# Preparation's inputs loaded one stage ahead, its order on VectorE and ScalarE anew, and the closing stage's selecting products behind its first tile

## The chip, the cores and the metric

The kernel runs on one core of one Trainium2 chip. The metric is the device time of one launch in microseconds, the median of several runs. Engines are named as in the profile: PE (TensorE matmul), PEld (its weight load), DVE (VectorE), ACT (ScalarE), POOL (GpSimd), SP (SyncE, which issues all DMAs here).

## What is computed

A mixture of experts, then three attention blocks, each added to its input `x`, which has 2 x 1024 rows of 256 floats.

```python
x = x + moe(x, cond_64, ...)                       # 8 experts, top 2, and 2 shared ones
x = x + rel_attn(x, mask_f, ..., null_kv=cond_64)  # layer 1
x = x + bias_attn(x, fside, mask_k, ...)           # layer 2
x = x + rel_attn(x, mask_f, ..., null_kv=cond_64)  # layer 3

def rel_attn(x, mask, ...):
    xn = ln(x, g_norm)
    q = l2norm(heads(xn @ Wq)) * q_scale           # 16 heads of 64
    k, v = split(xn @ Wkv)                         # one head of keys and values
    k, v = concat([null_k, k]), concat([null_v, v])
    k = l2norm(k) * k_scale
    h = silu(ln(pos @ w0 + b0, g0))                # a small network over 1024 distances
    h = silu(ln(h @ w1 + b1, g1)) @ w2 + b2        # gives the bias of each distance and head
    sim = q @ k.T * 8 + [null_attn_bias, h[i - j]]
    return ln(softmax(causal(sim, mask)) @ v @ Wout, g_out)
```

`bias_attn` is the same without the norms of q and k and without the small network: its bias is the input `fside`.

## The kernel before, in words

`program` (L2048) runs phases one after the other, each closed by a barrier of all engines: `moe_route`, `moe_experts`, and then for layers 1, 2 and 3 `prepare_layer`, `project`, `attend` and `close_layer`. Within a phase every engine has its own list of instructions, written out by hand, and semaphores order them; nothing of a phase starts before the slowest engine of the one before has reached the barrier. `Own` is a helper with which DVE waits for its own results.

`prepare_layer` (L583) makes what the projections need: the weights `Wq` and `Wkv` multiplied by `g_norm` (`fold` on ACT, L908; L737 on DVE), each split into a high and a low part (`wq_h` L911, `wq_l` L709, `wx_h` L761, `wx_l` L763); the products of `Wq` with the null key (`null_products`, L702) and their sums per head (`null_columns`, L758); the mask's penalty row (L726, L728); and the first 512 rows of `x` normalized, transposed and split (`first_rows` L828, `first_standardize` L841, `first_transposes` L694, L917, `first_low` L849). In layers 1 and 3 (`normed`) it also runs the small network over the 1024 distances, in quarters m = 0 to 3: two halves of the first layer, then two of the second. `distances` (L768) or `add_first_bias` (L774), `variances` (L781 to L788), `deviation` on ACT (L924), `offsets` (L793, L795), `normalize` on ACT (L932), transposes on PE (L989), `tangent` on ACT (L942), `silu` (L801), `high_silu` on ACT (L950), `low_silu` (L807), products on PE (L216). The last DVE instruction (L895) writes the bias row `brow`, SP stores it and issues the DMA that spreads it out in DRAM (L683), and the barrier follows.

Its inputs are loaded by SP at the phase's start (L646): 26 DMAs in a normed layer, 11 in layer 2. DVE's list starts with the first 512 rows of `x`, which need none of them.

`attend` (L1508) ends with DVE, ACT and PE idle and SP waiting until its stores of the attention's output, `o_dram`, have landed (L1660). The first of four chunks of that output has been loaded into `o_in` by then (`load_outputs`, L1501).

`close_layer` (L1851) multiplies the output by `Wout`: 16 tiles of 128 rows, four in a chunk. A tile: ACT makes the high part (L1914), DVE the low part (L1971), PE 48 products (L216), a transpose of the null weights (L1956), and one product for the null value (L1963), which needs ACT's copy of that transpose (L1932). ACT prepares tile n + 2 while PE is at tile n. That null product needs `null_out`, which comes from eight products with the raw `Wout` (`cl_vps`, L1943, the selecting products), the first thing that PE does in the phase. The raw `Wout` lies in the buffer of the second chunk, so SP waits for them before it loads chunk 1. It loads chunk c, from 2 on, when DVE has made the low parts of chunk c - 2, whose buffer it takes.

`moe_experts` (L387) loads the weights of two experts, then in a loop of four turns four blocks of `fside` (`load_corners`) that POOL masks (L514) between its low parts (L519).

## Time and profile before

| what | value |
|---|---|
| median of 3 runs | 2287.53 us (2285.26 to 2294.27) |
| the profiled execution | 2292.38 us, of which its span 2290.6 us |
| mean granted TensorE clock | 0.934 |
| PE busy | 1975.9 us (86%) |
| DVE busy | 1694.2 us (74%) |
| ACT busy | 1341.0 us (59%) |
| POOL busy | 1071.1 us (47%) |

Times of the trace are microseconds from the span's start. The phases that the change touches lie in these stretches: experts 32 to 219, preparation of the three layers 220 to 283, 936 to 960 and 1572 to 1635, closing stages 872 to 935, 1510 to 1571 and 2218 to the end. A row of a timeline has the start, the duration (of several instructions together where xN stands), engine, line, operation, the tiles written and read, and in brackets how long the engine was idle before it and what ended that.

### The profile page before, as it was taken

What the parts mean: (1) busy time and instruction counts of PE and PEld (TensorE: products, weight loads), DVE (VectorE), ACT (ScalarE), POOL (GpSimd) and SP (SyncE); (2) the same over time, 40 slices, a digit from 0 to 9 for tenths busy, and PEclk for the clock granted to TensorE, in tenths of its full rate; (3) what the DMA queues carried; (4) which work ended last, traced back from release to release, by engine and by line L of the source; (5) the groups of instructions that cost most, each with busy time, mean ns of one, the idle gap of its engine ahead of it and who ended that gap; (6) DMA issues with size and microseconds to landing.
All of it is one profiled execution on the core that took longest, in us unless ns stands there. A gap on an engine that the chain in (4) does not pass through costs nothing. (4 is left out here: it accounts for less than half of the span.)

```text
span 2290.6 us, 46788 instructions
## 1 busy us (share of the span) xinstructions
PE 1975.9 (86%) x11698; PEld 1428.0 (62%) x11698; DVE 1694.2 (74%) x4116; ACT 1341.0 (59%) x2908; POOL 1071.1 (47%) x1289
## 2 busy tenths in 40 slices
PE   5998496899999999488999999985686999999987
PEld 4886364666666668466666666675464666666667
DVE  5777767777887785657777877758487778887856
ACT  2222465677776674246766767643564777777753
POOL 1442113666765562105656666521123666666632
PEclk8999698899999999798999999997796999999999
DMA  3530167433333333286777877741464433343332
GB/s 114 170 129 18 47 212 254 118 112 111 111 112 110 100 113 120 77 315 195 240 230 237 240 239 238 230 157 39 142 217 161 125 111 110 111 121 114 111 111 98
DMA packets 220689, 338.83 MB, mean 148 GB/s; under 512 B 25910, under 2 KB 102844, under 8 KB 220508
## 3 DMA queue, kind: packets, MB, share of 16 engines
q1 hardware_dynamic: 220508, 336.86, 46.8%
q8 instruction: 60, 0.98, 0.2%
q14 instruction: 121, 0.99, 0.1%
HBM read 250.63 MB, written 102.91 MB: 154 GB/s over the span
## 5 line engine op out<-in xcount | busy, mean ns | idle before, releaser
L1569 POOL TENSOR_SCALAR at_row<-at_row,at_inv 128x129 f32<-128x129 f32 (+7 forms) x384 | 721.3, 1878 | 353.9 <-DVE at_inv L1731 346.5
L1778 ACT ACTIVATE at_row<-at_row,at_nmax 128x129 f32<-128x129 f32 (+7 forms) x768 | 595.4, 775 | 231.9 <-DVE at_nmax L1750 230.5
L1750 DVE CUSTOM_DVE_ANT_0 at_row<-at_s,bias,at_row 128x128 f32<-128x128 f32 (+7 forms) x768 | 618.4, 811 | 69.2 <-PE at_s L1678 38.0
L1690 PE MATMUL at_t<-ident,at_row 128*128 128x128 f32 x3456 | 546.1, 282 | 37.6 <-ACT at_pt L1771 32.6
L1690 PEld LDWEIGHTS at_t<-ident,at_row 128*128 128x128 f32 x3456 | 394.0, 142 | 242.4 <-issue 165.5
L1677 PE MATMUL at_s<-k_hh,q_hl 128*128 128x512 f32 (+3 forms) x1152 | 464.5, 403 | 47.6 <-SPq L1636 22.1
L1706 PE MATMUL at_o<-at_pt,v 128*64 128x512 f32 (+3 forms) x2304 | 442.5, 506 | 6.1 <-ACT at_pt L1771 2.5
L1584 DVE COPY at_pt<-at_t 128x128 f32<-128x128 f32 (+3 forms) x576 | 278.4, 483 | 188.7 <-PE at_t L1690 188.5
L1678 PE MATMUL at_s<-k_lp,q_h 65*128 65x512 f32 (+3 forms) x1152 | 393.6, 354 | 0.0
L1771 ACT ACTIVATE at_pt<-at_t 128x512 f32<-128x512 f32 (+2 forms) x576 | 306.8, 533 | 139.7 <-PE at_t L1690 134.0
L1677 PEld LDWEIGHTS at_s<-k_hh,q_hl 128*128 128x128 f32 x1152 | 226.3, 196 | 81.7 <-DVE at_nmax L1750 35.2
L1706 PEld LDWEIGHTS at_o<-at_pt,v 128*64 128x64 f32 x2304 | 144.7, 138 | 182.6 <-issue 146.3
L1569 DVE TENSOR_SCALAR at_row<-at_row,at_inv 128x129 f32<-128x129 f32 (+7 forms) x384 | 248.8, 648 | 0.9 <-DVE at_inv L1731 0.6
L1678 PEld LDWEIGHTS at_s<-k_lp,q_h 65*128 65x128 f32 x1152 | 226.7, 197 | 16.7
L1474 POOL TENSOR_TENSOR o_in<-pj_qn,o_in 128x512 fp32r<-128x512 f32 x38 | 52.7, 1390 | 213.3 <-ACT o_in L1233 213.3
L1778 ACT ACTIVATION_READ_ACCUMULATOR at_row<-at_row,at_nmax 128x1 f32 x768 | 143.9, 187 | 0.0
L1833 POOL COPY null_w<-at_row 128x2 f32 (+1 forms) x384 | 71.3, 186 | 137.3 <-DVE at_row L1569 74.3
L1821 POOL COPY at_row<-neg_null 128x2 f32 (+1 forms) x384 | 71.3, 187 | 126.5 <-DVEq L145 103.6
L519 POOL TENSOR_TENSOR moe_hid_l<-moe_hid,moe_hid_h 128x512 fp32r<-128x512 f32 x40 | 51.8, 1294 | 145.5 <-ACT moe_hid_h L504 145.5
L216 PE MATMUL cl_y<-wo_h,cl_oh 128*128 128x256 f32 x384 | 114.0, 297 | 0.0
L216 PE MATMUL cl_y<-wo_l,cl_oh 128*128 128x256 f32 x384 | 109.1, 284 | 0.0
L216 PE MATMUL cl_y<-wo_h,cl_ol 128*128 128x256 f32 x384 | 109.1, 284 | 0.0
(244 smaller groups left out, 2832.6 us busy)
## 6 DMA issues: line engine op xcount, KB each, us to landing
q_dram<-o_in SPq DMA_DIRECT2D x96, 512.0 KB, 3.7
q_hl<-q_dram SPq DMA_DIRECT2D x192, 256.0 KB, 4.4
bias<-bands_dram SPq DMA_DIRECT2D x64, 512.0 KB, 5.8
q_h<-q_dram SPq DMA_DIRECT2D x96, 256.0 KB, 5.2
o_dram<-at_o_sb SPq DMA_DIRECT2D x96, 256.0 KB, 4.7
o_in<-o_dram SPq DMA_DIRECT2D x10, 2048.0 KB, 8.6
bands_dram<-brow_dram SPq DMA_DIRECT2D x2, 8192.0 KB, 31.6
bias<-corners_dram SPq DMA_DIRECT2D x256, 64.0 KB, 4.3
```

The lines of the kernel that those rows point to most:

```text
L216: last = eng.matmul(out, left[a], right[b], start=start and n == 0, stop=stop and n == len(pairs) - 1)
L1569: return eng.tensor_scalar(cells, cells, inv[:, i:i + 1], None, ALU.mult)
L1584: copy(bass.AP(one.tensor, one.offset, [one.ap[0], [pitch, blocks], [1, P]]), t_ps[m % NTR][:, 0:blocks * P].rearrange("p (c i) -> p c i", ...
L1677: eng.matmul(out, q_hl[:, g % 2, side, at], t["k_hh"][:, b, c:c + n], start=True, stop=False)
L1678: last = eng.matmul(out, q_h1[0:DH + 1, g % 2, side, at], t["k_lp"][0:DH + 1, b, c:c + n], start=False, stop=True)
L1690: last = eng.transpose(t_ps[m % NTR][:, c * P:(c + 1) * P], row[:, u % RING, here:here + P], t["ident"][:])
L1706: last = eng.matmul(o_ps[side * DH:(side + 1) * DH, i0:BANK], t["v"][:, turn.half_of(GU * g) * NT + j, :], pt[g % 2][:, side, at + i0:at + ...
L1750: eng.tensor_tensor_reduce(out=row[:, u % RING, ZERO:ZERO + width], in0=s_ps[u % 2][:, 0:width], in1=bt[:, lo:lo + width], scale=-1.0, sca ...
L1771: return eng.activation(out, in_, ACT.Copy)
L1778: eng.activation(cells, cells, ACT.Exp, scale=-1.0, bias=nmax[:, i:i + 1], accum_out=rsum[:, i:i + 1]).then_inc(s["exp"], 1)
L1821: eng.tensor_copy(null_cell(u, 2), nulls(turn, "neg_null", u)).then_inc(s["null_in"], 1)
L1833: eng.tensor_copy(nulls(turn, "null_w", u), null_cell(u, 2)).then_inc(s["null_out"], 1)
```

## The change

1. `load_inputs` is new. SP issues the loads of the next `prepare_layer` from the phase before: those of layer 1 in `moe_experts`, between the first two experts' weights and the loop; those of layers 2 and 3 in `close_layer`, between the loads of chunk 1 and chunk 2. They go into the lower half of the bias buffer, which is allocated once for all layers now, and into small tiles of their own. `dist` is loaded once, in `moe_route`.
2. `prepare_layer`: ACT folds `Wq` first. DVE in layers 1 and 3 starts with the network, does the rows of `x` where it would wait for ACT's tanh, the mask, the null values and `wx` after the last `offsets`, and `null_columns` at the very end. The ones of `q_h1` (L862) are written in layer 1 alone, between `low_silu(2)` and `silu(3)`. In layer 2 the low part of `Wq` (L709) goes from DVE to POOL.
3. `close_layer`: the selecting products come behind PE's first tile, and the null product of tile 0 into the middle of tile 1.
4. `attend` doesn't wait for its last two stores; SP waits for them at the start of `close_layer`.

```diff
+def load_inputs(eng, t, w, cond, mask, layer):
+    i, normed = t["inputs"], layer != 2
+    def load(dst, src):
+        eng.dma_start(dst, src).then_inc(t["inputs_sem"], 16)
+        t["inputs_n"] += 16
+    if normed:
+        for n in ("w0", "b0"):
+            load(i[n], rows(w[n]))
+        for n in range(2):
+            load(i[f"g{n}"][:], w[f"g{n}"])
+        load(i["w1"], ...)
+        load(i["w2"][:], ...)
+        load(i["b2"][:], ...)
+        load(i["b1"], rows(w["b1"]))
+    load(i["wq"], w["Wq"].rearrange("(k p) n -> p k n", p=P))
+    load(i["gain"][:], w["g_norm"])
...
 # moe_experts, SP
                     load(eng, q, q)
+                load_inputs(eng, t, *inputs)
                 with eng.Fori(0, NU // PAR - 1) as it:
 # prepare_layer, POOL
             def _(eng):
+                loaded(eng)
                 if normed:
                     null_products(eng)
-                    low_part(eng)
+                low_part(eng)
 # prepare_layer, DVE
+                loaded(eng)
                 if not normed:
+                    null_square()
+                    first_rows()
+                    cleared()
+                    null_values()
+                    first_standardize()
+                    null_products(eng)
                     first_low()
-                    null_key()
-                    null_products(eng)
-                    low_part(eng)
                     null_columns()
                     xo.settle()
                     return
-                eng.wait_ge(s["rb_in"], 16 * 9)
+                null_square()
+                rb.step(eng.memset(w2[:], 0.0))
                 rb.settle()
+                rb.step(eng.tensor_copy(w2[:, :, 0:H], i["w2"][:]))
                 distances(0)
                 variances(0)
-                first_low()
                 distances(1)
+                offsets(0)
                 variances(1)
-                offsets(0)
                 offsets(1)
+                first_rows()
                 split_weights()
+                first_standardize()
                 silu(0)
                 low_silu(0)
                 silu(1)
                 low_silu(1)
+                first_low()
                 null_key()
-                for i in range(2):
-                    add_first_bias(i)
-                    variances(2 + i)
-                    offsets(2 + i)
+                rb.step(eng.memset(brow[:], -BIG))
+                add_first_bias(0)
+                variances(2)
+                add_first_bias(1)
+                offsets(2)
+                variances(3)
+                offsets(3)
+                cleared()
+                null_values()
+                for m in range(2):
+                    silu(2 + m)
+                    low_silu(2 + m)
+                    if m == 0:
+                        ones()
                 null_columns()
-                for i in range(2):
-                    silu(2 + i)
-                    low_silu(2 + i)
 # prepare_layer, ACT, layers 1 and 3
+                fold()
...
                 deviation(0)
+                normalize(0)
                 deviation(1)
-                normalize(0)
                 normalize(1)
+                first_deviation()
...
-                fold()
+                first_high()
+                high_part()
                 deviation(2)
+                normalize(2)
                 deviation(3)
-                normalize(2)
                 normalize(3)
 # attend, SP
-                    eng.wait_ge(s[f"o{g}"], 8 * NGRP * B * TURNS + 16)
+                    eng.wait_ge(s[f"o{g}"], 8 * NGRP * B * TURNS)
 # close_layer, SP
+                eng.wait_ge(t["o_stored"], t["o_stored_n"])
                 for c in range(1, NCH):
+                    if c == 2 and inputs is not None:
+                        load_inputs(eng, t, *inputs)
                     if c >= 2:
                         eng.wait_ge(s["o_lo"], CT * (c - 1))
                     else:
                         eng.wait_ge(s["null_mm"], 1)
 # close_layer, PE (null_rows: the eight selecting products; null_product: the product of L1963)
-                for a in range(NPAIR):
-                    last = eng.matmul(vps[:, 0:D], ...)
-                last.then_inc(s["null_mm"], 1)
                 for n in range(NTT):
                     eng.wait_ge(s["o_lo"], n + 1)
...
                         if a == NPAIR // 2:
+                            if n == 1:
+                                null_product(0)
                             eng.wait_ge(s["w_low"], 3)
...
+                    if n:
+                        null_product(n)
+                    else:
+                        null_rows()
```

Where the instructions stand, at the three places that the prediction speaks of. In rows of after, `bias` stands for the inputs and for the network's `h` and `z`, which all lie in that buffer.

DVE at the end of the preparation of layer 1, before, from the last statistics of the network on:

```order
L788 TENSOR_SCALAR rb_rstd<-rb_mv 128x4
L793 RECIPROCAL rb_rstd<-rb_rstd 128x4
L795 SCALAR_TENSOR_TENSOR rb_off<-rb_mv,rb_rstd 128x4
L758 TENSOR_REDUCE lw_wx<-lw_prod 128x16 x2
L761 CAST wx_h<-lw_wx 128x512
L763 TENSOR_TENSOR wx_l<-lw_wx,wx_h 128x512
L801 SCALAR_TENSOR_TENSOR o_in_4<-o_in_4,rb_tr_6 128x512 x2
L807 TENSOR_TENSOR rb_ul<-o_in_4,rb_uh 128x512 x2
L801 SCALAR_TENSOR_TENSOR o_in_4<-o_in_4,rb_tr_6 128x512 x2
L807 TENSOR_TENSOR rb_ul<-o_in_4,rb_uh 128x512 x2
L895 TENSOR_SCALAR rb_brow<-rb_mm,rb_b_6 16x1024
```

The same place after:

```order
L755 CAST lw_pen<-in_mask_0 2x1024
L757 TENSOR_SCALAR lw_pen_r<-lw_pen 2x1024
L761 COPY v0m<-in_v_0 64x8 x6
L766 TENSOR_SCALAR bias<-bias,in_gain 128x192 x2
L815 SCALAR_TENSOR_TENSOR o_in_0<-o_in_0,rb_tr_5 128x512 x2
L821 TENSOR_TENSOR rb_ul<-o_in_0,rb_uh 128x512 x2
L877 MEMSET q_h_0 1x512 x4
L815 SCALAR_TENSOR_TENSOR o_in_0<-o_in_0,rb_tr_5 128x512 x2
L821 TENSOR_TENSOR rb_ul<-o_in_0,rb_uh 128x512 x2
L772 TENSOR_REDUCE bias<-lw_prod 128x16 x2
L775 CAST wx_h<-bias 128x512
L777 TENSOR_TENSOR wx_l<-bias,wx_h 128x512
```

The mask and null values have come behind the last statistics, the memsets between the last two quarters, and the null columns (L758 to L763 of before, L772 to L777 of after) from ahead of the last silu to behind it.

PE at the start of the closing stage of layer 1, before (`cl_y0` is the result of tiles 0, 2, ..., `cl_y1` that of 1, 3, ...):

```order
L1706 MATMUL at_o_8<-at_pt1_8,v_4 64x128 x2
L81 UNCONDITIONAL_BRANCH
L1940 UNCONDITIONAL_BRANCH
L1943 MATMUL cl_vps_9<-o_in1_4,v0m_4 96x256 x8
L216 MATMUL cl_y0_9<-wo_h_4,cl_oh_9 128x256
L216 MATMUL cl_y0_9<-wo_l_4,cl_oh_9 128x256
```

After, the end of tile 0 and the start of tile 1:

```order
L216 MATMUL cl_y0_9<-wo_h_7,cl_oh_9 128x256
L216 MATMUL cl_y0_9<-wo_l_7,cl_oh_9 128x256
L216 MATMUL cl_y0_9<-wo_h_7,cl_ol_9 128x256
L1993 MATMUL cl_vps_9<-o_in1_0,v0m_0 96x256 x8
L216 MATMUL cl_y1_9<-wo_h_7,cl_oh_9 128x256
L216 MATMUL cl_y1_9<-wo_l_7,cl_oh_9 128x256
```

The eight selecting products now stand between tiles 0 and 1, and tile 0 is PE's first work of the phase.

SP in the closing stage of layer 1, before:

```order
L1505 DMA o_in_4<-o_dram 128x8x512
L1597 DMA o_dram<-at_o_sb 128x512 x4
L81 UNCONDITIONAL_BRANCH
L1884 UNCONDITIONAL_BRANCH
L1505 DMA o_in_4<-o_dram 128x8x512 x3
```

After:

```order
L1547 DMA o_in_0<-o_dram 128x8x512
L591 DMA bias<-in_L_Wq 128x2x1024
L591 DMA in_gain<-in_L_g_in 128x2
L591 DMA in_k_0<-in_cond 128x64
L591 DMA bias<-in_L_Wkv 128x2x64 x3
L591 DMA in_mask_0<-in_mask_k 2x1024
L591 DMA in_v_0<-in_cond 64x1 x2
L591 DMA null_bias<-in_L_null_attn_bias 128x16
L591 DMA gain_out_0<-in_L_g_out 128x256
L1547 DMA bias<-o_dram 128x8x512
```

The 11 loads of layer 2's inputs stand between those of chunk 1 and chunk 2; in the closing stage of layer 2 it is 25 of layer 3.

## Rows read from the trace of the kernel before

**Rows 1.** Windows: us, then busy us of each engine, granted clock, DMA.
```profile
1571.90:1630.60 58.70, 22.40 (x100) 18.76 (x100) 47.61 (x124) 27.95 (x48) 9.12 (x3) 0.60 0.14 38
935.90:958.30 22.40, 1.97 (x8) 1.57 (x8) 17.92 (x40) 5.39 (x6) 0.00 (x0) 0.50 0.22 64
872.20:877.40 5.20, 5.17 (x12) 3.52 (x13) 3.10 (x5) 2.31 (x3) 1.37 (x1) 0.50 0.00 0
```

**Rows 2.** Timeline of DVE in the preparation of layer 3.
```profile
1577.77 2.11 DVE L862 MEMSET q_h<- 1x512 f32 x4 [0.16 <-issue]
...
1594.98 1.28 DVE L801 SCALAR_TENSOR_TENSOR o_in<-o_in,rb_tr 128x512 f32<-128x512 f32 x2 [3.09 <-ACT o_in L942]
...
1608.57 1.81 DVE L795 SCALAR_TENSOR_TENSOR rb_off<-rb_mv,rb_rstd 128x4 f32<-128x4 f32 x1
...
1613.39 1.45 DVE L788 TENSOR_SCALAR rb_rstd<-rb_mv 128x4 f32<-128x4 f32 x1
...
1615.40 2.34 DVE L758 TENSOR_REDUCE lw_wx<-lw_prod 128x16 f32<-128x1024 f32 x2
...
1618.24 0.69 DVE L763 TENSOR_TENSOR wx_l<-lw_wx,wx_h 128x512 fp32r<-128x512 f32 x1
...
1629.25 1.27 DVE L895 TENSOR_SCALAR rb_brow<-rb_mm,rb_b 16x1024 f32<-16x1024 f32 x1 [2.75 <-PE rb_mm L216]
```

**Rows 3.** Timeline of POOL and ACT in the preparation of layer 3.
```profile
1605.70 4.65 POOL L702 TENSOR_TENSOR lw_prod<-lw_wq,lw_k0n 128x1024 f32<-128x1024 f32 x2 [40.68 <-ACT lw_wq L908]
1610.31 4.50 POOL L709 TENSOR_TENSOR wq_l<-lw_wq,wq_h 128x2048 fp32r<-128x2048 f32 x1
...
1614.99 4.03 ACT L932 ACTIVATE o_in<-o_in,rb_off,rb_rstd 128x256 f32<-128x256 f32 x8
...
1620.33 1.26 ACT L942 ACTIVATE o_in<-rb_tr,rb_half_g 128x512 f32<-128x512 f32 x2
```

**Rows 4.** Timeline of DVE in the preparation of layer 2.
```profile
945.26 0.68 DVE L726 CAST lw_pen<-lw_mask 2x1024 f32<-2x1024 uint8 x1 [0.99 <-DMA gain_out<-in_L_g_out]
...
947.26 0.55 DVE L737 TENSOR_SCALAR lw_wx<-lw_wx,lw_gain 128x192 f32<-128x192 f32 x2
...
950.22 2.36 DVE L702 TENSOR_TENSOR lw_prod<-lw_wq,lw_k0n 128x1024 f32<-128x1024 f32 x2 [2.31 <-ACT lw_wq L908]
952.50 2.29 DVE L709 TENSOR_TENSOR wq_l<-lw_wq,wq_h 128x2048 fp32r<-128x2048 f32 x1
```

**Rows 5.** Waits of SP: us in total, times, longest us.
```profile
SPq L1660 <- DMA o_dram<-at_o_sb: 4.2, 3, 1.5
```

**Rows 6.** Timeline at the start of layer 1's closing stage, rows of PE, DVE, SP, ACT.
```profile
881.47 0.28 PE L1963 MATMUL cl_y<-cl_null_out,cl_nwt 96*128 96x256 f32 x1
...
888.27 0.38 PE L1963 MATMUL cl_y<-cl_null_out,cl_nwt 96*128 96x256 f32 x1 [0.44 <-ACT cl_nwt L1932]
...
873.60 1.23 DVE L1971 TENSOR_TENSOR cl_ol<-o_in,cl_oh 128x1024 fp32r<-128x1024 f32 x1 [11.21 <-ACT cl_oh L1914]
...
878.69 18.00 SPq L1505 DMA_DIRECT2D o_in<-o_dram  x3
...
887.00 1.06 ACT L1914 ACTIVATE cl_oh<-o_in 128x1024 fp32r<-128x1024 f32 x1 [3.12 <-DMA o_in<-o_dram]
```

**Rows 7.** Timeline of SP: the last load of layer 3's inputs.
```profile
1584.64 0.43 SPq L646 DMA_DIRECT2D lw_wq<-in_L_Wq  x1
```

**Rows 8.** Timeline of SP, POOL and PE in the experts' first turn.
```profile
35.37 1.02 SPq L431 DMA_DIRECT2D moe_corner<-in_fside  x2
...
49.34 1.11 POOL L514 TENSOR_SCALAR_AFFINE_SELECT moe_corner<-moe_corner 128x1024 f32<-128x1024 f32 x1
51.09 1.30 POOL L519 TENSOR_TENSOR moe_hid_l<-moe_hid,moe_hid_h 128x512 fp32r<-128x512 f32 x1 [0.65 <-ACT moe_hid_h L504]
...
57.80 0.28 PE L216 MATMUL moe_down<-moe_wh,moe_hid_h 128*128 128x256 f32 x1
```

**Rows 9.** The page's issues of DMAs: KB each, median us to landing.
```profile
moe_corner<-in_fside SPq DMA_DIRECT2D x16, 512.0 KB, 6.4
```

More of the change, by code:

```diff
@@ L578, in _, with prepare_layer @@
                 eng.wait_ge(s["added"], TURN * (NU // PAR + 1))
-def prepare_layer(nc, t, w, cond, mask, normed):
-    names = ["in", "gain", "dve", "norm_in", "norm", "v0_in", "folded", "k0n", "prod", "hi", "lo"]
+def load_inputs(eng, t, w, cond, mask, layer):
+    i, normed = t["inputs"], layer != 2
+    VAL = 2 * DH
+    def load(dst, src):
[6 more added lines that the diff above has]
+            load(i[f"g{n}"][:], w[f"g{n}"])
+        load(i["w1"], w["w1"].rearrange("(k p) n -> p k n", p=P))
+        load(i["w2"][:], w["w2"].rearrange("(k p) n -> p k n", p=P))
+        load(i["b2"][:], w["b2"].rearrange("(n o) -> n o", o=1))
+        load(i["b1"], rows(w["b1"]))
+    load(i["wq"], w["Wq"].rearrange("(k p) n -> p k n", p=P))
+    load(i["gain"][:], w["g_norm"])
+    load(i["k0"][:], rows(cond[0, :]))
+    if normed:
+        load(i["kscale"][:], rows(w["k_scale"]))
+        load(i["qs"][:], rows(w["q_scale"]))
+        for c in range(2):
+            load(t["kscale"][c * DH:(c + 1) * DH, :], w["k_scale"].rearrange("(d o) -> d o", o=1))
+            load(i["qcol"][c * DH:(c + 1) * DH, :], w["q_scale"].rearrange("(d o) -> d o", o=1))
+    for at in (0, DH, VAL):
+        load(i["wx"][:, :, at:at + DH], w["Wkv"][:, at // VAL * DH:(at // VAL + 1) * DH].rearrange("(k p) n -> p k n", p=P))
+    load(i["mask8"][:], mask)
+    for c in range(2):
+        load(i["v0"][c * DH:(c + 1) * DH, :], cond[1, :].rearrange("(d o) -> d o", o=1))
+    load(t["null_bias"][:], rows(w["null_attn_bias"]))
+    load(t["gains_out"][layer % 2][:], rows(w["g_out"]))
+def prepare_layer(nc, t, layer):
+    normed = layer != 2
+    names = ["dve", "norm_in", "norm", "v0_in", "folded", "k0n", "prod", "hi", "lo"]
     names += ["pen", "pen_out", "x_dve", "x_var", "x_std", "x_norm", "x_tr", "x_hi", "x_lo"]
-    names += ["rb_in", "rb_dve", "var", "std", "offset", "normal", "tr", "tanh", "silu", "high", "low", "mm", "w_split", "half", "out"]
+    names += ["rb_dve", "var", "std", "offset", "normal", "tr", "tanh", "silu", "high", "low", "mm", "w_split", "half", "out",
+              "brow_out"]
     NS, HALF = 2, NT // 2
@@ L658, in _ @@
-                load("gain", gain[:], w["g_norm"])
-                load("gain", mask8[:], mask)
-                for at in (0, DH, VAL):
-                    load("gain", wx[:, :, at:at + DH], w["Wkv"][:, at // VAL * DH:(at // VAL + 1) * DH].rearrange(
-                        "(k p) n -> p k n", p=P))
-                load("gain", k0[:], rows(cond[0, :]))
-                for c in range(2):
-                    load("gain", v0[c * DH:(c + 1) * DH, :], cond[1, :].rearrange("(d o) -> d o", o=1))
@@ L666, in _ @@
-                if normed:
-                    load("gain", kscale[:], rows(w["k_scale"]))
-                    load("gain", qs[:], rows(w["q_scale"]))
-                    for c in range(2):
-                        load("gain", t["kscale"][c * DH:(c + 1) * DH, :], w["k_scale"].rearrange("(d o) -> d o", o=1))
-                        load("gain", qcol[c * DH:(c + 1) * DH, :], w["q_scale"].rearrange("(d o) -> d o", o=1))
-                load("gain", t["null_bias"][:], rows(w["null_attn_bias"]))
@@ L1596, in store @@
                     cols = slice((g % 2) * BANK, (g % 2 + 1) * BANK)
+                    last = place.known() and place.half == B - 1 and place.turn == TURNS and g + 2 >= 0
                     eng.dma_start(t["o_dram"][one, :, cols].rearrange("o p i -> p (o i)"), o_sb[:, g % 2, :]
-                                  ).then_inc(s[f"o{g % 2}"], 16)
+                                  ).then_inc(t["o_stored"] if last else s[f"o{g % 2}"], 16)
                 def queries(place, ready, g):
@@ new lines, in program @@
+            t["gain_out"] = t["gains_out"][layer % 2]
+            with tensors(nc) as (sbp, _):
+                t["xt_high"] = sbp("xt_high", [P, 2, KD, BANK], FR)
+                t["xt_low"] = sbp("xt_low", [P, 2, KD, BANK], FR)
+                for part in "hl":
+                    t[f"wq_{part}"] = sbp(f"wq_{part}", [P, KD, H * DH], FR)
+                    t[f"wx_{part}"] = sbp(f"wx_{part}", [P, KD, 2 * P], FR)
+                prepare_layer(nc, t, layer)
+                project(nc, t, normed, bias)
```

249 lines of the change are left out of this document (123 added, 126 removed).

## The prediction

> **What bounds the kernel now.** I read the windows by stage first, then the timelines of the engines in them, then the waits. Every phase ends at a barrier, so a phase costs what its slowest chain costs, and the average of PE (86% busy) says nothing about the stages that the change touches.
>
> Preparation. In layer 3, up to the end of the last DVE instruction, DVE is busy 47.61 of 58.70 us, PE 22.40 and POOL 9.12 [rows 1]: DVE sets the end. Its chain has three kinds of waste. It waits 3.09 us for the first tanh with work left that doesn't depend on it [rows 2]. It writes the ones of `q_h` on the path, 2.11 us, 2.27 with the gap before it [rows 2]. And two tiny instructions of 4 columns are drawn out: L795 takes 1.81 us and ends at 1610.38, where POOL's L702 ends (1610.35), and L788 takes 1.45 and ends at 1614.84, where POOL's L709 ends (1614.81) [rows 2, 3]. So while POOL runs its two long instructions, DVE instructions of some kinds are held until POOL is through: nearly all of these 3.26 us is waiting, some 2.9 in this phase. Behind the last statistics DVE has the null columns, 1615.40 to 1618.93 [rows 2], and these lie in the shadow of ACT's normalizing (4.03) and the tanh at 1620.33 [rows 3]. From the start of that tanh to L895 is 8.92 us, to its end 10.19. Layer 1 runs alike; layer 2 is shorter, DVE 17.92 of 22.40 us [rows 1].
>
> Attention's end. SP alone waits, 4.2 us over the three layers, for the last stores to land [rows 5].
>
> Closing. PE is the busy engine, but its start is a chain of buffers: selecting products, then SP's load of chunk 1 at 878.69 (6.5 us after the phase's start at 872.20), then ACT, which waits 3.12 us for that load until 887.00, and then tile 2's null product at 888.27, for which PE waited 0.44 [rows 6]. PE runs at a granted clock of 0.50 up to 877.40 [rows 1], which is the 1.2 GHz level, and at full clock behind it.
>
> **The change part by part.** Times in parentheses with + count from the phase's start.
>
> 1. Route: one more DMA on SP, `dist`, ahead of the loads of `x`. A small load costs SP 0.43 us [rows 7]: **+0.4**.
>
> 2. Experts. SP has 25 input loads in front of the corner loads. In preparation the same loads, 26 of them, occupy it from 1571.90 to 1585.07 [rows 1, 7], 0.51 us each, so the corner loads move from 35.37 to about 48.1 [rows 8] and land 6.4 us later [rows 9], at 54.5 by the median. POOL then masks (1.11) and makes its low part (1.30), which ends at about 56.9 instead of 52.4. PE takes that low part with its `moe_down` products at 57.80 [rows 8]. So it is hidden, by 0.9 us: **0**. If the cover is gone PE is late by what the landing is late; upper bound 4.6, the whole delay of the low part, the lower bound 0, since nothing leaves this phase.
>
> 3. Preparation of layer 3. Off DVE's chain ahead of the last quarters' tanh go: the ones, 2.27; the wait for tanh, 3.09, now filled by the first rows of `x` [rows 2]; mask, null values and `wx`, in layer 2's rows from 945.26 to 947.81, 2.5 us [rows 4], which move into the shadow of normalizing and tanh, where the null columns were; and half of ACT's normalizing, since quarter 2 is now normalized before the statistics of quarter 3 are there, half of 4.03, 2.0 [rows 3]. Together 9.9. The small memsets that go into the shadow as well and the small steps that come in front (the null key's square, a padded copy of `w2`, `brow`) are each some 1 us by instructions of this size, and I put them against each other. Behind the last low part come the null columns, 3.53 long. DVE waited there for PE's products, 2.75 [rows 2], so 0.8 shows. POOL's two instructions start behind the null key as before and meet the same kinds of instruction; I take the 2.9 us as unchanged. 9.9 less 0.8: **-9.1**. Bounds: -12 if POOL's long instructions no longer meet such an instruction, -6 if the first tanh is still waited for.
>
> 4. Preparation of layer 1: the same, but the ones stay and stand between two quarters, behind the last statistics, where DVE is the chain: -9.1 + 2.27 = **-6.8**.
>
> 5. Preparation of layer 2. Of 17.92 busy the ones (2.11) and the low part (2.29, to POOL) go; of 4.48 idle the wait for the folded weights (2.31) and for the mask's loads (0.99) [rows 1, 4]. What is left is 13.5 and 1.2, an end at +14.7 instead of +22.4. But the low part costs POOL 4.50 [rows 3], from about +4.3 (ACT's fold and high part, 5.39 busy in all less small ones) to +8.8, and DVE reaches L737, a tensor_scalar like L788, at about +5.2. If it is held, it ends at 8.9 instead of 5.7, and everything behind it with it: 22.4 - 14.7 - 3.3, **-4.4**. The bounds are -7.7 (not held) and -3.8 (the copies ahead of it held too).
> The Trainium skill, page "SBUF — State Buffer", section "Who interferes with whom", says that VectorE and GpSimd share a port pair under a lock that is held for a whole instruction, and that copies and tensor_scalar in the fast modes need it. By it the copies would be held too, and this sum would be 0.6 less favourable; the long L788 and L795 of the trace agree with the lock, and no row here shows a copy held.
>
> 6. Attention's end: SP's wait for the last stores moves to the start of the closing stage, ahead of the load of chunk 1. Only that load is queued behind it, and it waits for the selecting products by far longer. So 1.4 x 3: **-4.2** [rows 5].
>
> 7. Closing stages. Tile 0 needs its low part, which DVE ends at 874.83 (+2.6) [rows 6]; before, the selecting products filled this time, now PE is idle. The selecting products took until 878.69, tile 0 from there to 881.47, 2.8 us at full clock [rows 6]. Measured in time at full clock, the 5.2 us at half clock [rows 1] are 2.6, the rest to 878.69 is 1.3, so selecting is 3.9 and tile 0 2.8, 6.7 together. After: if PE again spends 5.2 us at half clock, from +2.6 to +7.8, 2.6 of 6.7 is done, and the remaining 4.1 end at **+11.9**. Only then is chunk 1 loaded, 5.4 later than before. The load took 8.3 to free ACT (878.69 to 887.00), then 1.3 to the null product of tile 2 [rows 6]: +21.5 instead of +16.1. PE has done its two tiles by then and waits, so the 5.4 us is lost in full, as the cover of 0.44 shows: PE was already waiting for this load. For three layers: **+16.3**. Bounds for one layer: +2.7 (clock up as early as before), +6.5 if 5.4 is joined by slower transfers.
>
> 8. Input loads in the closing stages stand ahead of chunk 2. In layer 2's, 25 loads of 0.51 behind +12 put its load at +25; it lands 8.3 later, +33.3. ACT wants it four tiles of about 3.1 us behind chunk 1, at +20.2 + 12.4 = +32.6: **+1.0**, bounds 0 and +5. In layer 1's it is only 11 loads: 0.
>
> Sum: +0.4 + 0 - 9.1 - 6.8 - 4.4 - 4.2 + 16.3 + 1.0 = **-6.8 us**. Against the profiled execution that is 2292.4 - 6.8 = 2285.6. That execution lies 4.9 above the median of 2287.5, which the sum takes to **2280.7**.
>
> **The rivals.**
> A. DVE isn't held by POOL (or the new order dodges it). Against it: L795 and L788, which end with POOL's instructions [rows 2, 3]. For it: the instructions that meet POOL are others now. It gives 3.3 and twice 2.9 more: -15.9, **2271.6**.
> B. The clock rises sooner in the closing stages. Before, it rose 5.2 us after PE's first selecting product; PE's first work is now tile 0's, of another kind, and full clock could be granted from about +5.2, as before: the products would be through at +9.2 rather than +11.9, 2.7 in each layer, 8.1: -14.9, **2272.6**. Against: PE was busy for 5.17 of the 5.20 us at the low level [rows 1], so the start of its work, not that of the phase, is the likelier thing to count from.
> C. Slower than before: the inputs' loads get in the way of large ones. Each is small, in many short pieces, and they share the DMA engines with the 2 MB load of chunk 1 in layers 1 and 2 and with the corner loads. If each of these lands some 5 us later there is no cover (0.9 in the experts, none behind ACT's wait for chunks): +5 +5 +4.6 on the sum, +7.8, **2295.3**. From 7 us in total it decides the sign. For it: PE already waits for chunk 1 and the cover is nil. Against: they are issued behind that load, when most of it is under way.
> The Trainium skill, "DMA: Bandwidth & Descriptors", section "Specifications", wants 512 bytes or more in a descriptor for line rate; that speaks for C, and no run yet shows by how much.
> D. The preparation gains don't come, since the end of the chain is ACT or PE after the reordering: -20.3 becomes about -12, 2289.
>
> **How the numbers follow.** Forecast 0.62 (its own range 2274 to 2289), A 0.08, B 0.12, C 0.12, D 0.04, none of them 0.02. The predicted time is the forecast's, 2280.7. The range runs from 2270, a little below A, to 2297, a little above C. 0.5% is 11.4 us, about what a measurement of this kernel tells from no change: faster is below 2276.1, slower above 2298.9. A, B and a small part of the forecast's range lie below, 0.23; above lies only C with longer delays, 0.04; the rest, 0.73, is between.
>
> **What would show it.** Step 3 and 4: L895 of before, the last DVE instruction, ends at about +49.5 in layer 3 and +51.7 in layer 1, no idle time for the first tanh. Step 5: DVE ends at about +18, with one tensor_scalar of `wx` over 3 us long that ends with POOL's low part; under A it is 0.5 and the end +14.7. Step 6: no wait of SP at the attention's end. Step 7: PE starts at +2.6 with the clock at 0.50 up to about +7.8, the selecting products end at about +11.9 (B: +9.2), and ACT waits over 8 us for chunk 1. Step 8: in layer 2 ACT waits about 1 us at chunk 2. Step 2: PE isn't idle ahead of `moe_down` in the first turn. The forecast is wrong if the closing stages lose less than 3 or more than 7 us each, or if one preparation gains under half of its term.

## The result, and the profile after

The changed kernel takes 2293.38 us in the median of 20 runs (2289.02 to 2304.48), the kernel before 2287.97 us (2281.57 to 2294.66, 20 runs). The ratio is 1.0031, with a 95% interval from 1.0018 to 1.0043. By the ratio the change costs 7 us (the two medians differ by 5.4), where 6.8 us of gain was forecast.

The profiled execution of the changed kernel took 2289.02 us, its span 2287.2, and so lies at the fast end of its runs, while the profiled execution of the kernel before (2292.38) lies above its median. The two traces alone would say -3.4 us. So I compare them stage by stage. Each number is in us and runs from the first instruction of a stage to the first of the next. Two borders are drawn otherwise: a projection begins with its first instruction on ACT (PE starts on its products up to 3 us earlier, and these are counted to the preparation), and the last stage ends with its last DVE instruction.

| stage | before | after | forecast of the difference | measured |
|---|---|---|---|---|
| route | 31.3 | 31.6 | +0.4 | +0.3 |
| experts | 188.2 | 189.1 | 0 | +0.9 |
| preparation 1, 2, 3 | 62.8, 26.7, 62.8 | 55.2, 23.2, 52.9 | -6.8, -4.4, -9.1 | -7.6, -3.5, -9.9 |
| projection 1, 2, 3 | 118.4, 70.0, 118.4 | 118.1, 69.6, 118.6 | 0 | -0.3, -0.4, +0.2 |
| attention 1, 2, 3 | 470.8, 477.3, 464.5 | 467.0, 471.3, 464.9 | -1.4 each | -3.8, -6.0, +0.4 |
| closing 1, 2, 3 | 63.7, 62.1, 68.4 | 68.2, 77.9, 75.1 | +5.4, +6.4, +5.4 | +4.5, +15.8, +6.7 |

The preparation came as forecast, to within 1 us a layer. The closing stages lose 27 us instead of 17, and the attention stages, whose code differs only in their last wait, scatter by more than that wait is worth. The granted clock goes with it: the trace of before has TensorE at the lower level of the granted clock for 74.6 us of its three attention stages, that of the changed kernel for 47.9. Without them the measured differences add up to +6.7 us, and with the 4.2 us at which the wait was priced to +2.5.

The preparation of layer 3, where [rows 1] had DVE busy for 47.61 of 58.70 us, and that of layer 2 (columns as in [rows 1]):

```profile
1571.80:1620.60 48.80, 23.39 (x100) 19.40 (x100) 45.59 (x121) 27.71 (x48) 9.19 (x3) 0.59 0.00 1
929.80:948.80 19.00, 1.97 (x8) 1.57 (x8) 18.02 (x35) 5.28 (x6) 4.51 (x1) 0.50 0.00 0
```

DVE is busy for 45.6 of 48.8 and for 18.0 of 19.0 us: the waits are gone. Below, the rows of DVE in layers 3 and 2 that answer to [rows 2, 4], and POOL's:

```profile
1587.03 1.29 DVE L815 SCALAR_TENSOR_TENSOR o_in<-o_in,rb_tr 128x512 f32<-128x512 f32 x2
...
1598.44 0.76 DVE L802 TENSOR_SCALAR rb_rstd<-rb_mv 128x4 f32<-128x4 f32 x1
...
1600.44 3.21 DVE L809 SCALAR_TENSOR_TENSOR rb_off<-rb_mv,rb_rstd 128x4 f32<-128x4 f32 x1
...
1619.27 1.27 DVE L926 TENSOR_SCALAR rb_brow<-rb_mm,in_b 16x1024 f32<-16x1024 f32 x1
...
934.30 4.94 DVE L761 COPY v0m<-in_v 64x8 f32<-64x8 f32 x6
...
1599.13 4.50 POOL L717 TENSOR_TENSOR wq_l<-bias,wq_h 128x2048 fp32r<-128x2048 f32 x1
...
934.22 4.51 POOL L717 TENSOR_TENSOR wq_l<-bias,wq_h 128x2048 fp32r<-128x2048 f32 x1 [10.81 <-ACT wq_h L941]
```

The first `silu` no longer waits for tanh, nor does the last DVE instruction wait for PE. L809 (before: L795) is drawn out to 3.21 us and ends at 1603.65, where POOL's low part ends (1603.63). In layer 2 it is the six small copies of the null value that are held, 4.94 us instead of 0.64, until POOL is through at 938.73; the tensor_scalar behind them takes its 0.55.

The second closing stage, which starts at 1493.96; the issues of SP, the first tile of each chunk on ACT, and PE's null products of tiles 0 to 2 and 6:

```profile
1506.05 0.40 SPq L1547 DMA_DIRECT2D o_in<-o_dram  x1
1506.50 0.57 SPq L591 DMA_DIRECT2D bias<-in_L_w  x1
...
1522.05 0.43 SPq L591 DMA_DIRECT2D gain_out<-in_L_g_out  x1
1522.52 0.43 SPq L1547 DMA_DIRECT2D bias<-o_dram  x1
...
1514.57 1.06 ACT L1962 ACTIVATE cl_oh<-o_in 128x1024 fp32r<-128x1024 f32 x1 [5.44 <-DMA o_in<-o_dram]
...
1532.83 1.06 ACT L1962 ACTIVATE cl_oh<-bias 128x1024 fp32r<-128x1024 f32 x1 [5.03 <-DMA bias<-o_dram]
...
1507.89 0.36 PE L2003 MATMUL cl_y<-cl_null_out,cl_nwt 96*128 96x256 f32 x1 [0.51 <-ACT cl_nwt L1980]
1509.63 0.28 PE L2003 MATMUL cl_y<-cl_null_out,cl_nwt 96*128 96x256 f32 x1
1515.83 0.39 PE L2003 MATMUL cl_y<-cl_null_out,cl_nwt 96*128 96x256 f32 x1 [2.93 <-ACT cl_nwt L1980]
...
1534.10 0.58 PE L2003 MATMUL cl_y<-cl_null_out,cl_nwt 96*128 96x256 f32 x1 [3.87 <-ACT cl_nwt L1980]
```

Chunk 1 is loaded at +12.1, as forecast. The 25 input loads then occupy SP for 16.0 us, not 12.7, chunk 2's load goes out at +28.6 instead of +25, and it lands 10.3 us later instead of 8.3. ACT waits 5.03 us for it, where 1.0 was forecast. And behind both waits of PE here, and behind its wait for chunk 1 in the third closing stage, there is a stretch at the lower level of the granted clock (0.5, 1.2 GHz):

```profile
1516.10:1519.60 3.50, 3.50 (x17) 3.44 (x17) 2.41 (x4) 1.16 (x3) 0.00 (x0) 0.51 0.91 325
1533.20:1540.10 6.90, 6.00 (x27) 5.96 (x28) 4.66 (x7) 3.56 (x7) 1.09 (x1) 0.51 0.41 151
2229.50:2233.00 3.50, 3.50 (x17) 3.50 (x17) 2.34 (x4) 1.20 (x3) 0.00 (x0) 0.51 0.90 338
```

PE is busy there, so by my estimate 3.5 us at half clock are 1.7 us of delay and 6.9 us some 3. It isn't a rule: the first closing stage has a wait of 2.66 us for chunk 1 that ends at 882.12, and the clock stays at 1.00 behind it. The second closing stage of the kernel before had no such stretch behind its first 3 us. These were in no term of the sum.

### The profile page after: what moved, and what is told of

It is laid out like the page before. It is cut to its first block and busy times, and to the rows that moved or that the text cites. A ratio compares the mean times of both kernels' runs of the same rounds, so it can differ in the third digit from the quotient of the medians.

```text
span 2287.2 us, 46777 instructions
## 1 busy us (share of the span) xinstructions
PE 1977.3 (86%) x11698; PEld 1432.3 (63%) x11698; DVE 1687.9 (74%) x4109; ACT 1339.9 (59%) x2908; POOL 1072.6 (47%) x1290
## 5 line engine op out<-in xcount | busy, mean ns | idle before, releaser
L1721 PE MATMUL at_s<-k_hh,q_hl 128*128 128x512 f32 (+3 forms) x1152 | 463.0, 402 | 48.1 <-SPq L1679 21.9
L1750 PE MATMUL at_o<-at_pt,v 128*64 128x512 f32 (+3 forms) x2304 | 436.7, 501 | 5.9 <-ACT at_pt L1815 2.5
L1721 PEld LDWEIGHTS at_s<-k_hh,q_hl 128*128 128x128 f32 x1152 | 225.3, 196 | 83.1 <-DVE at_nmax L1794 33.8
L216 PE MATMUL cl_y<-wo_h,cl_oh 128*128 128x256 f32 x384 | 120.5, 314 | 16.0 <-DVE cl_ol L2031 16.0
L1877 POOL COPY null_w<-at_row 128x2 f32 (+1 forms) x384 | 71.2, 186 | 130.9 <-DVE at_row L1611 69.6
L1516 POOL TENSOR_TENSOR o_in<-pj_qn,o_in 128x512 fp32r<-128x512 f32 x26 | 36.1, 1392 | 177.7 <-ACT o_in L1275 177.7
L216 PE MATMUL cl_y<-wo_l,cl_oh 128*128 128x256 f32 x384 | 114.1, 297 | 0.0
L216 PE MATMUL cl_y<-wo_h,cl_ol 128*128 128x256 f32 x384 | 113.8, 296 | 0.0
```

What stands on the lines that cost most here:

```text
L216: last = eng.matmul(out, left[a], right[b], start=start and n == 0, stop=stop and n == len(pairs) - 1)
L1721: eng.matmul(out, q_hl[:, g % 2, side, at], t["k_hh"][:, b, c:c + n], start=True, stop=False)
L1750: last = eng.matmul(o_ps[side * DH:(side + 1) * DH, i0:BANK], t["v"][:, turn.half_of(GU * g) * NT + j, :], pt[g % 2][:, side, at + i0:at + ...
L1877: eng.tensor_copy(nulls(turn, "null_w", u), null_cell(u, 2)).then_inc(s["null_out"], 1)
```

## The experiments

The names of the kernels: what begins with a_ is made from the changed kernel, b_ from the kernel before.

**The changed kernel once more.** No edit.

> The changed kernel itself, once more. It has 2293 us in the median but 2289.0 in its profiled execution, and the kernel before 2288 and 2292.4. If the closing stages carry the loss (68.2, 77.9, 75.1 us, together 27 more than before) and the attention stages only scatter, the closing and preparation stages repeat within 0.5 us, the three attention stages differ by some us from the first trace, and the ratio to before is 1.003 again. If the second closing stage was an accident of that execution, it comes out near 70 us.

2297.74 us median; ratio to before 1.0035 (1.0019 to 1.0050). The preparation stages are 55.2, 23.2 and 52.9 us, within 0.01 of the first trace. The closing stages are 68.0, 76.1 and 74.1, so the second and third are 1.8 and 1.0 off where 0.5 was expected, but the second was no accident. The attention stages are 467.4, 473.4 and 466.0, up to 2 us off the first trace. Its profiled execution is the fastest again, at 2289.74.

**The order on PE taken back.**

```diff
+                null_rows()
                 for n in range(NTT):
...
-                            if n == 1:
-                                null_product(0)
...
-                    if n:
-                        null_product(n)
-                    else:
-                        null_rows()
+                    null_product(n)
```

> The changed kernel with the selecting products ahead of tile 0 again and tile 0's null product at its end; nothing else is different. Theory (the order of the closing stage sets it): chunk 1 is loaded from about +6.3, the first and third closing stages fall from 68.2 and 75.1 to the 63.7 and 68.4 us of before, the second from 77.9 to about 67, since its inputs still stand ahead of chunk 2's load: -22 us, 2271. Rival (the input loads and the moved wait cost it, not the order): the three stages fall by under 2 us each, 2288.

2273.71 us, ratio 0.9937 (0.9916 to 0.9958). The closing stages are 60.9, 72.4 and 67.4 us. The first and third fell by 7, more than to the level of before; the second by 5.5 only. Most of what is left there stands in its rows: chunk 2 is issued at 1511.45, 17 us behind chunk 1, and ACT waits for it. Some 3 us are of another kind: the granted clock is 0.50 in the first 4 us of this stage, and chunk 1 goes out at +6.8, in a_both below at +3.8.

```profile
1494.06 0.40 SPq L1547 DMA_DIRECT2D o_in<-o_dram  x1
1511.45 1.46 SPq L1547 DMA_DIRECT2D bias<-o_dram  x1
...
1520.90 1.06 ACT L1962 ACTIVATE cl_oh<-bias 128x1024 fp32r<-128x1024 f32 x1 [6.54 <-DMA bias<-o_dram]
```

**The input loads behind all chunks.**

```diff
                 for c in range(1, NCH):
-                    if c == 2 and inputs is not None:
-                        load_inputs(eng, t, *inputs)
...
+                if inputs is not None:
+                    load_inputs(eng, t, *inputs)
```

> The changed kernel with the next layer's input loads issued behind chunk 3's load in the closing stages, ahead of nothing; the order of PE is that of the changed kernel. Theory (25 issues on SP in front of chunk 2's load cost the second closing stage 8 us beyond the later chunk 1): that stage falls from 77.9 to about 69.5, the first stays at 68.2, total -8, 2285. Rival (the transfers of the inputs get in the way of a chunk, wherever they stand): the second stays above 74 and a chunk behind them lands late, 2291.

2293.01 us, ratio 1.0011 (0.9994 to 1.0028). The second closing stage fell to 70.1 us, the first and third are 67.7 and 74.5. Chunk 2 is no longer late, and the preparation behind is as short as in the changed kernel (52.9), so the loads fit behind chunk 3. The ratio moved by 0.24 points against that of a_again, 5.5 us, with intervals that overlap; the traces say 6 to 8.

**Both.**

> Both edits: selecting products first, input loads behind chunk 3's. What is left of the change is the preparation with its loads one stage ahead, and the wait for the last stores. Theory (these are the gain and the closing stage the whole loss): closing stages 63.7, 62.1, 68.4 us as before, preparation stages at 55.2, 23.2 and 52.9 as in the changed kernel, -27 against it: 2266, ratio to before 0.991. Rival (part of the preparation's gain is only waiting that moved into the stages behind it): projection or attention stages are longer by as much, and the total stays above 2275.

2264.71 us, ratio 0.9901 (0.9880 to 0.9922). Closing stages 60.8, 61.3 and 67.2 us, preparation 55.2, 23.2 and 52.9, projection unchanged (118.3, 69.7, 118.1). The whole loss was the closing stage. Its two causes: against a_both the tile order alone costs 6.9, 8.8 and 7.3 us (a_inputs_late), the inputs ahead of chunk 2 alone 11.1 in the second stage (a_rows_first, with the 3 us of its slow start in them), the two together 16.6 there, less than the two added.

The first two closing stages are shorter than in the kernel before, by 2.9 and 0.8 us, though PE's list is that of before. The windows of their first 4 us, before, and then a_both:

```profile
872.20:876.20 4.00, 3.97 (x10) 2.72 (x11) 2.60 (x5) 2.31 (x3) 1.37 (x1) 0.50 0.00 0
```

```profile
864.70:868.70 4.00, 3.95 (x20) 3.16 (x21) 2.58 (x5) 2.56 (x4) 1.38 (x1) 1.00 0.00 0
```

The clock granted is 1.00 instead of 0.50, and the selecting products are through at +3.8 instead of +6.5. The next run asks why.

**The wait for the last stores, put back.** It is a_both with

```diff
                 t["o_stored_n"] += 32
+                eng.wait_ge(t["o_stored"], t["o_stored_n"])
```

> a_both with SP's wait for the last stores back at the end of attention, so that the preparation with its early loads is all that differs from the kernel before. Theory (the moved wait is worth more than its 1.4 us a layer: TensorE stands still for less time ahead of the closing stage, keeps full clock, and is through with the selecting products at +3.8 instead of +6.5): attention stages 1.4 us longer, the first two closing stages back to about 63.7 and 62.1 from 60.8 and 61.3, 4.2 + 4 us slower than a_both, 2272. Rival (only the wait itself): closing stages as in a_both, +4.2, 2269.

2268.25 us, ratio 0.9928 (0.9913 to 0.9942). The first two closing stages are 62.6 and 64.1 us, longer by 1.7 and 2.8 than a_both's; the third, 67.6 and 67.2, hardly differs. First a_both's selecting products, then this one's, and the window of its first 4 us:

```profile
864.75 3.67 PE L1993 MATMUL cl_vps<-o_in,v0m 128*96 128x256 f32 x16 [2.77 <-PEq L83]
```

```profile
864.56 5.35 PE L1994 MATMUL cl_vps<-o_in,v0m 128*96 128x256 f32 x16 [3.98 <-PEq L83]
```

```profile
864.50:868.50 4.00, 3.94 (x11) 2.71 (x12) 2.56 (x5) 2.31 (x3) 1.38 (x1) 0.61 0.00 0
```

With the wait PE stands idle for 3.98 us ahead of the closing stage, without it for 2.77, and in these two traces the first 4 us are then at 1.00 instead of 0.61. But the shorter idle time doesn't always keep the clock up. a_low_dve, described below, has a_both's closing stage and the same 2.77 us ahead of it:

```profile
865.52 5.35 PE L1994 MATMUL cl_vps<-o_in,v0m 128*96 128x256 f32 x16 [2.77 <-PEq L83]
```

```profile
865.50:869.50 4.00, 3.98 (x11) 2.72 (x12) 2.61 (x5) 2.31 (x3) 1.35 (x1) 0.57 0.00 0
```

In a_best, below too, both of the first two closing stages start so, at 0.63 and 0.50 after 2.75 and 2.85 us. Over the five kernels that have the selecting products first and no wait for the stores (a_rows_first, a_both, a_hold_order, a_best, a_low_dve), 6 of the 10 first and second closing stages have full clock over their first 4 us; of the 4 with the wait (this kernel and the kernel before) none does. The third starts at the lower level in all of them, even after 2.43 us. And the four with a_both's closing stage take 60.7 to 62.2 us for the first and 61.0 to 64.3 for the second, so 62.6 and 64.1 hardly stand out. The attention stages, expected 1.4 us longer, are 468.4, 474.5 and 466.1 against a_both's 468.5, 475.2 and 465.9. That the wait costs more than its 1.4 us is therefore not shown. This kernel, the preparation with early loads and nothing else, is worth 0.72%, or 16 us.

**The order on PE on the kernel before.** 

```diff
-                for a in range(NPAIR):
-                    last = eng.matmul(vps[:, 0:D], ...)
-                last.then_inc(s["null_mm"], 1)
...
+                            if n == 1:
+                                null_product(0)
...
+                    if n:
+                        null_product(n)
+                    else:
+                        null_rows()
```

> The kernel before with the closing stage's new order on PE alone (selecting products behind tile 0). By the prediction's sum this is worth +5.4 in each layer, +16 in all, 2304. By what the changed kernel's stages show against a_both (+6.9, +8.9, +7.3) it is +23, 2311. Rival (the loss is one of the new order together with the early loads): under +8.

2307.37 us, ratio 1.0113 (1.0094 to 1.0131): 26 us slower. In the traces the stages are 70.2, 67.8 and 74.6 us, +6.5, +5.8 and +6.2, together 18.4, near the +16.3 of the prediction. The ratio of the runs says 7 us more than these three stages; the profiled execution is the fastest of its six. The mean granted clock of the six is 0.933, that of the profiled one 0.936, that of the runs of before 0.937.

**Products in PE's wait.** In the changed kernel, ahead of tile 2's null product:

```diff
+                    if n == 2:
+                        for k in range(24):
+                            eng.matmul(vps[0:ROWS, 0:D], t["wo_h"][:, k % NPAIR, 0:ROWS], t["wo_l"][:, k % NPAIR, :],
+                                       start=True, stop=True)
```

> The changed kernel with 24 more products on PE (their result is not used) ahead of tile 2's null product, where PE waits 3 us for chunk 1. Theory (the wait lets the granted clock fall, which was not in the prediction): the low stretch at +20 to +25 of the second and third closing stages is gone and these stages are 1.7 us shorter each, although PE does more; median -3 to -4 against the changed kernel, 2290, and less scatter of its executions. Rival (the low stretch comes from something else): it stays where it is, and the stages keep 76 to 78 and 74 to 75 us.

2294.14 us, ratio 1.0044 (1.0031 to 1.0057), not distinct from the changed kernel's 1.0031. The places behind the first wait of PE in stages 2 and 3, and behind later waits:

```profile
1516.50:1520.50 4.00, 3.79 (x30) 3.42 (x29) 2.87 (x5) 2.99 (x7) 0.00 (x0) 1.00 0.92 323
1534.00:1541.00 7.00, 5.74 (x26) 5.70 (x27) 4.17 (x7) 3.92 (x7) 0.68 (x1) 0.53 0.63 232
2229.50:2233.50 4.00, 4.00 (x33) 3.72 (x32) 3.17 (x5) 2.98 (x7) 0.00 (x0) 1.00 1.01 374
2257.90:2264.90 7.00, 5.01 (x23) 4.97 (x24) 3.46 (x6) 3.93 (x7) 1.25 (x1) 0.51 0.23 75
```

The first low stretch is gone in both; it was there in these two stages of every trace of the changed kernel and of a_inputs_late. So PE's idleness in the wait for chunk 1 brought it there, though it doesn't always: b_tile_first waits 2.36 us in its second stage and keeps full clock. But the stages are 68.0, 76.6 and 74.6 us: the low stretch at a later wait lasts 6.8 us now, where it lasted 3.4 in the third stage (2260.20 to 2263.70) of the changed kernel. The expected 1.7 us a stage was found in neither. That the start of the stage was part of it is open.

**Layer 2's list in another order.** a_both, with `first_standardize`, the null products and their sums ahead of the mask and the null values:

```diff
                     cleared()
-                    null_values()
                     first_standardize()
                     null_products(eng)
+                    null_sums()
+                    null_values()
                     first_low()
-                    null_columns()
+                    null_parts()
```

> a_both with DVE's list of layer 2's preparation in another order: the copies of the null value, which took 4.94 us while POOL made its low part, come behind the null products and their sums, so that what meets POOL is a product of two SBUF tiles, a reduction and a standardization. Theory (POOL holds one-input copies and tensor_scalar instructions, not products and sums): the stage falls from 23.2 to about 19.5 us, since only a tensor_scalar started before +4.3 can be touched, -3.7, 2261. Rival (every DVE instruction that meets POOL's is held): 23.2 again, with the hold on the products.

2264.57 us, ratio 0.9918 (0.9904 to 0.9932), which can't be told from a_both; in the trace the stage fell from 23.2 to 20.4.

```profile
929.85 2.35 DVE L710 TENSOR_TENSOR lw_prod<-bias,lw_k0n 128x1024 f32<-128x1024 f32 x2
932.24 2.35 DVE L772 TENSOR_REDUCE bias<-lw_prod 128x16 f32<-128x1024 f32 x2
934.50 2.61 DVE L755 CAST lw_pen<-in_mask 2x1024 f32<-2x1024 uint8 x1
...
929.59 6.98 POOL L717 TENSOR_TENSOR wq_l<-bias,wq_h 128x2048 fp32r<-128x2048 f32 x1 [11.11 <-ACT wq_h L950]
```

The products and the sums run beside POOL at their usual 2.35 us. But now POOL pays: its low part takes 6.98 us instead of 4.51, and the cast that meets its end is held for 2 us. Half of the theory was right.

**Layer 1's loads behind the experts' loop.** a_hold_order, with `load_inputs` moved:

```diff
-                load_inputs(eng, t, *inputs)
                 with eng.Fori(0, NU // PAR - 1) as it:
...
                         store_corners(it, j)
+                load_inputs(eng, t, *inputs)
```

> a_hold_order with layer 1's input loads behind the experts' loop instead of ahead of it. Theory (the loads in front of the corner loads let POOL's low part come 0.9 us after PE wants it): the experts' phase falls from 188.9 to the 188.2 of before, the wait of 1.99 us ahead of moe_down in the first turn is gone, the preparation of layer 1 still finds its inputs there and stays at 55.2: -0.8 us against a_hold_order, ratio to before 0.991. Rival (the loads then land too late for the preparation): that stage is longer by what they lack.

2259.72 us, ratio 0.9897 (0.9878 to 0.9916), the fastest of all, though its interval overlaps a_both's and a_low_dve's. PE's wait ahead of `moe_down`, 1.21 us in a_hold_order, is gone, and the preparation still takes 55.2. But the phase is 189.0 us, as in a_hold_order, and the clock rises at the same point of it in both, at about +11 us (+9.5 in the kernel before). That the loads in the experts' phase cost time isn't shown.

**Layer 2's low part on DVE.** a_both, with

```diff
 # POOL
                 if normed:
                     null_products(eng)
-                low_part(eng)
+                    low_part(eng)
 # DVE, layer 2
                     first_low()
+                    low_part(eng)
                     null_columns()
```

> a_both with the low part of layer 2's Wq on DVE again (2.3 us there, ahead of the null columns) instead of on POOL (4.5 us). Theory (POOL holds DVE's copies for 4.3 us, so moving the low part costs more than it saves): the copies take 0.64 us again, the stage is 23.2 - 4.3 + 2.3 = 21.2 us, -2.0 against a_both. By the prediction, which had only the tensor_scalar held for 3.3 us, -1.0. Rival (the copies are long for another reason): they stay at 4.9 us and the stage grows to 25.5.

2260.14 us, ratio 0.9900 (0.9875 to 0.9924). The stage is 21.1 us, -2.1, and the copies take 0.63 us. So sending the low part to POOL cost 2 us more than it saved; in the total that is under what these runs resolve.

## Why the prediction was wrong

The sum was 14 us off (-6.8 against +7), and the direction with it. What failed are the terms of steps 7 and 8, the closing stages. The runs divide the sum in two: a_both has what steps 1 to 6 price, -24.1 us forecast, and measured -23 (its interval goes from -27 to -18). Steps 7 and 8 were +17.3, and between a_both and the changed kernel lie 1.3%, some 30 us. About 25 of these belong to the order on PE (+16.3 forecast) and about 5.5 to the input loads (+1.0 forecast). Step by step:

1. **Route**: right, +0.3.

2. **Experts**, forecast 0 with cover of 0.9: the cover was gone. The corner loads went out at 50.35, not 48.1, and the first mask ran at 56.41. The expected wait of PE is there:

```profile
50.35 5.76 SPq L432 DMA_DIRECT2D moe_corner<-in_fside  x4
...
56.41 1.10 POOL L516 TENSOR_SCALAR_AFFINE_SELECT moe_corner<-moe_corner 128x1024 f32<-128x1024 f32 x1 [6.76 <-DMA moe_corner<-in_fside]
57.47 1.26 POOL L521 TENSOR_TENSOR moe_hid_l<-moe_hid,moe_hid_h 128x512 fp32r<-128x512 f32 x1
...
58.87 0.38 PE L216 MATMUL moe_down<-moe_wh,moe_hid_h 128*128 128x256 f32 x1 [1.99 <-POOL moe_hid_l L521]
```

It takes the place of one of 1.20 us (ahead of `moe_gate`, at 54.91 before), and the phase is 0.9 longer, though a_best, where the wait is gone, was no shorter.

3. and 4. **Preparations 3 and 1**: right. -9.9 and -7.6 for -9.1 and -6.8; the last DVE instruction of layer 3 ends at +48.7, forecast +49.5. The order's gain and the size of POOL's hold (3.6 us, taken as 2.9) came as worked out. Nothing of it was given back later: a_stores_waited keeps it.

5. **Preparation 2**: -3.5 for -4.4, a little outside the bounds (-7.7 to -3.8). The hold was there, but on the copies, not on the tensor_scalar behind them. Here the sentence in the prediction on the page "SBUF — State Buffer" of the Trainium skill, section "Who interferes with whom", was the better guide: copies in the fast modes need the shared port too, and this trace agrees, with 4.94 us for copies that take 0.64.

6. **Attention's end**: the wait is gone. PE's idle time ahead of the three closing stages is 3.93, 3.99 and 3.94 us in the kernel before and 2.77, 2.85 and 2.43 in a_both, 3.8 us less in all, for -4.2. In the run times it is 6 us by the middle of a_stores_waited's and a_both's ratios, with intervals that overlap; a price beyond the 4.2 isn't shown. The changed kernel adds 2.65 us of idleness to each again, since PE's first work there waits for the low part of tile 0.

7. **Closing stages**: the mechanism was right and the point of time too. The selecting products end at +10.9, +12.1 and +11.7 (forecast +11.9), and PE waits for chunk 1. In the traces the size is near as well: against the kernel before, +18.4 in b_tile_first for +16.3. In the run times the term was some 9 us too small: 26 us for b_tile_first, and 1.1% or 25 us between a_inputs_late and a_both. Only a part of the difference can be seen. PE's wait for chunk 1 was at 0.44 us and grew to between 2.3 and 3.1, and in 8 of the 12 stages with this order (three each in the changed kernel, a_again, a_inputs_late and b_tile_first) a stretch at half clock follows, mostly worth 1.7 us, which the sum had at nothing. And against a_both, whose first two closing stages start at full clock, the traces give 23 us. The other microseconds are in executions of which there is no trace.

8. **Inputs ahead of chunk 2**: the step furthest off for its size, +1.0 forecast, 7.7 us in the second stage (77.9 against 70.1 in a_inputs_late) and 5.5 in the run times. Three things were each too small: 0.64 us for the issue of a load in this stage instead of 0.51, 10.3 us to land instead of 8.3, and again the stretch at half clock behind PE's wait, 6.9 us long. The first two make chunk 2 late by 5.0 us (ACT wants it at +33.8 and has it at +38.9), the third adds some 3. A cover of nearly nothing (+32.6 wanted, +33.3 there) had been written down as a cost of nearly nothing; every microsecond of lateness counted in full.

**The rivals.** A (no hold by POOL) is excluded by L809 and L761. B (clock up sooner, at about +5.2) came near in one stage of three: in this trace the clock rose at +5.9, +8.6 and +7.8, and the selecting products ended about when the forecast had them. C had the right sign and nearly the right total (+7.8), but that the totals agree is luck, since its mechanism is only in part what happened: the corner loads were late by SP's issue, chunk 1 wasn't late at all (8.5 us from issue to ACT's use in the second stage, 8.3 before), and chunk 2 was late for its issue above all, with 2 us more in its transfer. Whether those 2 us are due to the small packets of the inputs wasn't tried. D (the preparation's gain doesn't come) is excluded by the stages' lengths.

What stays open: why the run times lose more to the new order on PE than the closing stages of the traces do, some 7 us in b_tile_first. Among the 21 runs of the kernel before beside a_again, time and mean granted clock go together (2284.82 us at 0.936, 2297.37 at 0.932), so the clock is where I would look. Among the twelve traces the time at the lower level in the attention stages alone varies from 47.9 to 74.6 us, and their three lengths together from 1401.3 to 1412.5. In which stages a slower execution loses can't be seen without a trace of it.

## What to carry to other kernels

A queue's place in the order is a resource like any other: before work is sent ahead on it, look for what stands behind it with no cover, and price an overrun of a thin cover by the bounds, not by the middle. Where an engine starts a stage with something that others wait for, a rearrangement that lets it begin 2.6 us later and puts another piece of work ahead costs the whole chain behind it; here that order was worth 1% of the kernel. And a change of many parts is to be taken apart: a_both, which keeps the preparation and the moved wait, takes the order on PE back and issues the input loads behind all chunks, beats both kernels by 1% or more. That the preparation is worth 0.7% by itself is shown; what the moved wait adds is not resolved.

## What the runs showed of the hardware that was not expected

- Idle time of PE can have a second price, half clock behind it, and even short idle times can: stretches of 3.4 to 6.9 us at half clock followed waits of 2.4 to 4.1 us inside the closing stages of the changed kernel's two traces, but not those of 2.66 and 2.78 us in the first of these stages. Ahead of the first two closing stages, 2.75 to 2.85 us of idleness left full clock in 6 of 10 stages, 3.93 to 3.99 us in none of 4.
- POOL and DVE interfere both ways. POOL's `TENSOR_TENSOR` over 128x2048 took 4.51 us beside held DVE copies and 6.98 us beside DVE's product of two SBUF tiles and a reduction, which weren't slowed (2.35 us each).
- Issuing a small load costs SP about half a microsecond: in the kernel before, 26 took 13.3 us at the start of layer 3's preparation (0.3 to 0.6 each), and in the second closing stage of the changed kernel 25 took 16.0 us, up to 0.85 for one.
